# Two EGAT layers on one core: who gathers seven tiles of source rows in layer 2

## What is computed

```python
def _egat_conv(x, e, src, dst, W_ni, W_nj, W_fij, W_node, attn):
    f = (x @ W_ni.T)[src] + (x @ W_nj.T)[dst] + e @ W_fij.T
    f = leaky_relu(f, 0.2)
    score = f @ attn
    a = exp(score - segment_max(score, dst)[dst])
    a = a / segment_sum(a, dst)[dst]
    h = x @ W_node.T
    h_out = segment_sum(h[src] * a[:, None], dst)
    return h_out, f

h0, h1 = _egat_conv(x, e, src, dst, ...)          # layer 1
h0, h1 = relu(h0) + x, relu(h1) + e
h0b, _ = _egat_conv(h0, h1, src, dst, ...)        # layer 2
out = layernorm(x + h0b + x)
```

## Time and profile before

| | |
|---|---|
| time, median of three runs | 2155.59 us (2153.46 to 2156.14) |
| span of the profiled execution | 2849.0 us |
| PE busy in the span | 2104.0 us (74%) |
| GpSimd busy, nearly all in 1655 indirect transfers | 1576.3 us (55%) |
| VectorE busy | 1455.7 us (51%) |
| ScalarE busy, issuing not counted | 673.3 us (24%) |
| single-row transfers of ScalarE | 896 of 1 KB |
| mean granted clock of PE | 0.790 |

### The profile page before, as it was taken

One profiled execution on the slowest core, in us unless ns is written; L12 is line 12 of the kernel. 1 busy time (PEld: TensorE's weight loads), 2 busy tenths in 40 slices (PEclk: granted clock), 3 DMA queues, 4 the chain that ended last, 5 costly groups with the idle time before them and its releaser, 6 DMA issues.

```text
span 2849.0 us, 46360 instructions
## 1 busy us (share of the span) xinstructions
PE 2104.0 (74%) x10659; PEld 1469.1 (52%) x10816; DVE 1455.7 (51%) x5358; ACT 673.3 (24%) x1260; POOL 1576.3 (55%) x1664
## 2 busy tenths in 40 slices
PE   2377878777787778887854887776777877678778
PEld 2235555555555555555632555554555555455556
DVE  3334655555554555555721555554545555455556
ACT  0243333333333333333300111111111111111112
POOL 7326666666665656556263455555555556555650
PEclk7688887888787787787956877787877778778788
DMA  6646677666766666767543455555555555555551
GB/s 187 193 150 196 209 212 209 206 211 206 211 202 205 198 202 198 206 199 210 184 117 93 138 158 155 151 159 148 160 154 152 156 158 159 151 144 157 161 159 44
DMA packets 352361, 489.15 MB, mean 172 GB/s; under 512 B 115220, under 2 KB 217925, under 8 KB 352093
## 3 DMA queue, kind: packets, MB, share of 16 engines
q1 hardware_dynamic: 236803, 249.78, 29.2%
q0 software_dynamic: 78416, 212.69, 26.2%
q10 hardware_dynamic: 37017, 25.40, 3.0%
HBM read 409.00 MB, written 81.38 MB: 172 GB/s over the span
## 4 chain that ended last, share of the span: by engine, by line
PE 25%; another core or an unknown queue 23%; issue 21%; DVE 11%; ACTq 10%; ACT 4%; SPq 3%; DMA 1%; DVEq 1%
ACTq L755 6%; PE bSC L906 6%; PE pair L865 6%; PE pair L917 6%; DVE amat L1243 3%; PE pair L886 2%; ACTq L751 2%; DVE fT L1389 2%; ACT zc L715 1%; ACT onehot L767 1%; DVE h L1392 1%; PE pair L890 1%; ACT onehot L761 1%; SPq L438 1%
## 5 line engine op out<-in xcount | busy, mean ns | idle before, releaser
L585 POOL DMA_INDIRECT xsrc<-h_table,idx_slot x804 | 766.6, 953 | 562.3 <-issue 207.6
L585 POOL DMA_INDIRECT xsrc<-x_table,idx_slot x767 | 726.0, 947 | 551.7 <-issue 234.6
L906 PE MATMUL bSC<-fT,attn_at 128*32 128x128 f32 x3328 | 541.9, 317 | 204.7 <-DVE fT L1389 86.8
L715 ACT ACTIVATE zc<-pair 128x512 f32<-128x512 f32 x416 | 248.2, 597 | 1841.2 <-remote 1007.3
L865 PE MATMUL pair<-edge_in,wts 128*128 128x512 f32 x832 | 580.4, 785 | 23.4 <-issue 13.3
L917 PE MATMUL pair<-amat,xsrc 128*128 128x42 f32 x3328 | 532.2, 315 | 51.8 <-issue 49.8
L917 PEld LDWEIGHTS pair<-amat,xsrc 128*128 128x128 f32 x3328 | 497.0, 225 | 121.8 <-issue 110.1
L906 PEld LDWEIGHTS bSC<-fT,attn_at 128*32 128x32 f32 x3328 | 384.5, 127 | 304.4 <-issue 181.7
L1389 DVE TENSOR_TENSOR fT<-pair,zc 128x512 f32<-128x512 f32 x416 | 285.8, 687 | 423.7 <-ACT zc L715 219.7
L886 PEld LDWEIGHTS pair<-ident,xsrc 128*128 128x128 f32 x1600 | 251.3, 170 | 330.4 <-issue 328.7
L1243 DVE TENSOR_SCALAR amat<-iota_row,relc,wcol 128x42 f32<-128x42 f32 x1568 | 378.8, 319 | 14.8 <-DVE numT L1227 0.2
(11 more groups left out here) (170 smaller groups left out, 1408.9 us busy)
## 6 DMA issues: line engine op xcount, KB each, us to landing
edge_in<-eT SPq DMA_DIRECT2D x208, 256.0 KB
rel_bc<-relrow_g SPq DMA_DIRECT2D x416, 128.0 KB
h1T<-h SPq DMA_DIRECT2D x208, 256.0 KB
edge_in<-h1T SPq DMA_DIRECT2D x208, 256.0 KB
stage<-h_table ACTq DMA_DIRECT2D x896, 1.0 KB
window<-proj SPq DMA_DIRECT2D x416, 32.0 KB
xsrc<-h_table,idx_slot POOLq DMA_INDIRECT x824
xsrc<-x_table,idx_slot POOLq DMA_INDIRECT x767
```

Source lines behind the costliest of these rows:

```text
L585: pool.indirect_dma_start(xsrc[b][:, i, 0:width], None, table, bass.IndirectOffsetOnAxis(ap=idx_slot[b][:, i:i + 1], axis=0)).then_inc(L.g ...
L715: nc.scalar.mul(zc[s][:, :], bZ[s][:, :], SLOPE).then_inc(L.z_scaled, 1)
L906: last = mm(bSC[0:TC, 0:P], attn_at[:, L.n - 1, TC - 1 - t:2 * TC - 1 - t], fT[s][:, i * P:i * P + P], start=t == 0, stop=t == TC - 1)
```

## The change

GpSimd gathers all 32 tiles of every chunk in layer 2 too; `aided_rows`, its tiles, its index input and its semaphores are gone, PE's wait for a group has one form again, and ScalarE's loop goes over one chunk at a time, 21 times round, in both layers.

```diff
-AIDED = (CH - XB) // XB
-AID_AT = 2 * XB - 1
-ROWS_AT = [5, 7, 5, 6, 7, 6, 6, 7]
-def first_row(turn, g):
...
# GpSimd
-                        aided = L.n == 2 and not isinstance(c, int) and b == AID_AT % XB and g == GC - 1
-                        for i in range(g * TG, g * TG + TG - (SHORT if ends else aided)):
+                        for i in range(g * TG, g * TG + TG - (SHORT if ends else 0)):
# ScalarE
-                    if L.n == 2 and aid is not None:
-                        aided_rows(*aid, c, g)
-
-                def aided_rows(turn, u, begins, c, g):
...
-                turn(1, True, True, (2, -1, True))
-                turn(2, True, True, (0, 0, False))
-                turn(3, True, True, (1, 0, False))
-                with act.Fori(0, AIDED - 1) as j:
-                    turn(j * XB + 4, True, True, (2, j, True))
-                    turn(j * XB + 5, True, True, (0, j + 1, False))
-                    turn(j * XB + 6, True, True, (1, j + 1, False))
-                c = (AIDED - 1) * XB + 4
-                turn(c, True, True, (2, AIDED - 1, False))
-                for c in range(c + 1, CH):
+                for c in range(1, 4):
                     turn(c, True, True)
+                with act.Fori(4, CH - 1) as c:
+                    turn(c, True, True)
+                turn(CH - 1, True, True)
# PE
-                        elif L.n == 2 and b == AID_AT % XB and g == GC - 1:
-                            above(pe, L.aided_in, rounds * 16)
-                            pe.sem_inc(pe_passed, 1)
-                            earlier = (L.uses_before[b] + 1) * (16 * TG)
-                            pe.wait_ge(L.gathered[b][g], rounds * (16 * (TG - 1)) + earlier)
```

More of the change, by code:

```diff
@@ L40 @@
 SHORT = NT - TILES
-AIDED = (CH - XB) // XB
-AID_AT = 2 * XB - 1
-IN_RANGE = "src lies in [0, N)"
-ROWS_AT = [5, 7, 5, 6, 7, 6, 6, 7]
-def first_row(turn, g):
-    before = 0 if turn == 0 else ROWS_AT[GC - 1] + (turn - 1) * sum(ROWS_AT)
-    at = before + (0 if turn == 0 else sum(ROWS_AT[0:g]))
-    return at, max(0, min(ROWS_AT[g], P - at))
 class Layer:
@@ L99, in __init__ @@
         self.slab_stored = sem(f"slab_stored{n}")
-        self.line_in = sem(f"line_in{n}") if h1_out is None else None
-        self.rows_in = sem(f"rows_in{n}") if h1_out is None else None
-        self.aided_in = sem(f"aided_in{n}") if h1_out is None else None
         self.proj_stored = sem(f"proj_stored{n}") if h1_out is not None else None
@@ L141, in above, with program @@
         eng.wait_ge(sem, value)
-def program(nc, eT, xT, xrows, idxC, idxR, idxE, dstT, dstC, dst8, ends, w_fij1, w_ni1, w_nj1, w_node1, attn1,
+def program(nc, eT, xT, xrows, idxC, idxE, dstT, dstC, dst8, ends, w_fij1, w_ni1, w_nj1, w_node1, attn1,
             w_fij2, w_ni2, w_nj2, w_node2, attn2, out):
@@ L204, in program @@
         window = [sb(f"window{g}", [P, 3 * TG, P], bf16) for g in range(GS // 2)]
-        stage = sb("stage", [P, 2 * P])
-        line = sb("line", [1, P], i32)
         rel_bc = [sb(f"rel_bc{g}", [P, W], bf16) for g in range(GS)]
@@ L295, in program @@
         pe_passed, dve_passed, pool_passed = sem("pe_passed"), sem("dve_passed"), sem("pool_passed")
-        sp_passed, act_passed = sem("sp_passed"), sem("act_passed")
+        sp_passed = sem("sp_passed")
         const_in = sem("const_in")
@@ L706, in layer, with slot @@
             def layer(L, narrow):
-                def slot(c, g, front, soft, aid):
+                def slot(c, g, front, soft):
                     n, s = c * GC + g, g % 2
@@ L773, in copy_rows, with turn @@
                     nc.scalar.copy(xsT[s][:, :], bXT[:, :]).then_inc(L.xt_copied, 1)
-                def turn(c, front, soft, aid=None):
+                def turn(c, front, soft):
                     for g in range(GC):
-                        slot(c, g, front, soft, aid)
+                        slot(c, g, front, soft)
                 def whole_slab(k):
@@ L1489 @@
         "idxC": t(srcp.reshape(CH, TC, P).transpose(0, 2, 1)),
-        "idxR": t(srcp.reshape(CH, TC, P)[AID_AT:AID_AT + XB * AIDED:XB, TC - 1, :]),
         "idxE": t(srcp.reshape(CH, TC, P)[XB - 1, 0:SPEC].reshape(1, SPEC * P)),
```

## The result

The changed kernel takes 2166.4 us (median of four runs, 2162.8 to 2169.8) against 2155.9 for the kernel before in the same comparison; the ratio is 1.0043, with a 95% interval of 1.0030 to 1.0057. The medians differ by 10.6 us; the ratio gives 9.3 us, with an interval of 6.5 to 12.3. The forecast was 2163 us, in a range of 2144 to 2169. On two of the four chips that the experiments met, the kernel before takes about 2830 us (the long condition, mean granted clock of PE 0.78 to 0.80) instead of about 2155 (the usual condition, clock mostly 0.93 to 0.94), and the trace of the kernel before that stands above has the span and the clock of the long one. The changed kernel's profile was taken in the usual condition: its span of 2160.6 us agrees with its time.

A forecast was written before the change was run, and what follows sets the result against it. GpSimd's gathers were taken to pace both layers in the timed runs; seven more at 1.14 us add 8.0 to 2155.6, all else nothing, giving 2163.6, forecast as 2163 us since a part may hide; range 2144 to 2169, its own 2160 to 2167.

The forecast's parts named there:

- What bounds the kernel: Both layers, timed runs: GpSimd's gathers set the pace almost without a wait, four taking 4.56 us against 3.98 a slot.
- The duration of a gather: GpSimd's seven added gathers in layer 2: 1.14 us each, 8.0 us in all; 6.7 at 0.953, 8.3 at 1.179.
- ScalarE's work, counted at nothing: Removing 147 register loads and 896 rows, 551 us on ScalarE, saves nothing, hidden by the wait for GpSimd's rows.
- The loop's laps at nothing: ScalarE's loop, 21 laps instead of 6 in each layer: taken as nothing, bounded above by 123 us.
- The instruction fetch at the jump back: ScalarE's layer 2 loop refetches code at jump backs; the change removes six stops, some 4.1 us each, priced under faster.
- Rival A: Layer 2: other engines pace it too, so the seven gathers vanish in GpSimd's waits: 2155.6 us; chance 0.19.
- Rival B: Layer 2: ScalarE paces the slots between one `zc` and the next, so the change is faster, 2139 to 2118; chance 0.18.
- What would show it: Profile after: 831 gathers, no `stage` transfers, `zc` own-queue waits in layer 2 from 476 to below 50 us, no instruction packets.

The follow-up runs named there:

- the new trace: Kernel before, unedited, run once more for a profile in the usual condition: 2152.3 us, span 2150.1.
- all four comparisons with additional gathers: Changed kernel 1.0043; same gathers with ScalarE's row work kept 1.0041; changed kernel with ScalarE's three-chunk loop without rows 1.0049; changed kernel plus 21 gathers in layer 2 1.0155.
- rows and gathers: Kernel before with all ScalarE row work kept, but its tile copied to an unused place and GpSimd gathering all tiles: 2163.3 us, ratio 1.0041.
- left out: Changed kernel, but GpSimd leaves out the seven layer 2 tiles and nobody fetches them: 2153.9 us, ratio 1.0003.
- the pair at 29 gathers: 63 tiles left out of layer 2's gathers, long condition: changed kernel without rows 2720.0 us, 0.9623; kernel before with ScalarE's rows 2784.5 us, 0.9863.
- 21 left out: Changed kernel, but GpSimd leaves out the last tile of all 21 loop chunks in layer 2, fetched by nobody (1641 gathers): ratio 0.9910.
- the whole table: Seven kernels with 1641 to 1683 gathers against the kernel before, from 21 fewer than the changed kernel to 21 more: ratios 0.9910 to 1.0155.

## Why the prediction was right, point by point

- **What bounds the kernel.** Right in the usual condition, and the step that carried it was to hold the trace against the timed runs: 1655 gathers nearly fill the timed 2155.6 us, and the slots can run faster than four of them. The profile's own chain and waits did not show it, since they were taken in the other condition.
- **The duration of a gather.** The mechanism was right and this term mis-sized: "If those stretches keep their length, it takes at most 1.139 us" was no bound, since the idle stretches did not shrink by a quarter but from 192.5 to 17.9 us, the stretch behind the last gather from 74.4 to 44 us, and the gather kept its 1.25. That the gathers fill the time did not need a shorter gather: 1655 x 1.25 = 2069 us and the 66 us of such stretches that are left make 2135 of the 2150 us of the new trace. The value of 1.14 and the end at 1.179 are both too low; the trace's own 1.25, which I had put down as the upper end, is right, 7 x 1.25 = 8.8 us instead of 8.0. The forecast took off another 0.6 us for waits that might hide a part; no run shows such a part. The measured 2166.4 is within the forecast's own range of 2160 to 2167, and all four comparisons with additional gathers have 1.25 us within their intervals. That the wrong value did so little harm is due to the small number of gathers: seven times 0.11 us is less than the interval.
- **ScalarE's work, counted at nothing.** Right in the usual condition, by two pairs: rows and gathers against the changed kernel (1.0041, 1.0043), left out against before (1.0003). The cover is thicker than reckoned: the slot is 5.0 us, not 4.56. One argument for it was weak: that the slots of layer 2 are only 0.10 us longer than those of layer 1, "which have none". In layer 1 ScalarE makes the one-hots, twice 0.71 us a slot, so the two layers do not compare, and in the condition of that trace the work did cost time.
- **The loop's laps at nothing.** Right within a few us: 1.0049 and 1.0043 with 6 and 21 laps.
- **The instruction fetch at the jump back.** Right as an observation and without a price here: between 1300 and 1900 us the kernel before again has 35 instruction packets of that queue and the changed kernel none, and a stop is 4.1 us, yet the time does not show the six of them. In the reading of the earlier trace rows the prediction says that of 6.4 us of lateness 3.4 are for rows still to be issued; from 2021.1 to 2023.4 it is 2.3, and with that the 4.1 us come out.

```profile
q14 instruction: 35, 0.29, 0.1%
```

- **Rival A**, hidden: wrong, gathers count in both directions. **Rival B**, faster: wrong in the usual condition. On the chips in the long condition the change gains 0.8%, 22 us, and ScalarE's work costs time there (64 us in the pair at 29 gathers), as this rival said. Its price of 17 to 38 us takes in the 22; how much of it is stops at the jumps back and how much the rows' own issuing was not separated.
- **What would show it.** 811 + 20 gathers and no transfers to `stage`: so. `zc` on its own queue below 50 us in layer 2: so in the usual condition, where the waits of that stretch have no such row; in the long one it is 121.1. The ground, that a gather less in each chunk moves the time by about 1.1 us for each, holds as well: 1.39 for the 21 left out, 1.26 over the whole table. The shorter span came, but from the condition: in the long one the changed kernel still spans 2811.2 us.

What stays open: why some chips take 2830 us for a kernel that takes 2155 on others, and what sets the pace there. PE's granted clock is 0.79 in the mean instead of 0.94, and GpSimd waits 2 to 3 us at a time for PE's sums. No experiment was made on the cause.

No version that beats the kernel before came out of this. ScalarE could collect more than seven tiles only if its slot allowed it (0.6 + 1.5 + 2.8 = 4.9 us of 5.0 with seven rows), and sharing such rows with SP, or a smaller number in layer 1, was not tried.

## What to carry to other kernels

Before reading a profile's chain, set its span against the timed runs. Where they differ by a third, as here, the chain can be that of another condition; what one engine must do in all, held against the timed total, is then the better guide. Where one engine issues at a fixed rate almost without a pause, seven instructions less are worth seven times its period, and 580 us of work on a neighbour with room cost nothing as long as each slot's share fits. A gain bought that way can turn into a loss in another condition. And an engine that is missing from the chain may still not be free: that takes a run with fewer of its instructions to see.

## What the runs showed of the hardware

- GpSimd issues an indirect transfer of 128 rows every 1.25 us where nothing holds it (0.95 and a gap of 0.30), with rows of 512 bytes (a mean of 1.00 and the same gap) or 1 KB, and in both conditions of the chip, at a mean granted clock of PE of 0.79 and of 0.94.
- Loading five to seven registers from an index row took ScalarE 1.5 us in the median (0.7 to 2.5) in the usual condition, a single-row transfer 0.40 us (seven in 2.77); a tile of 128 rows costs it 83 us (21 x 1.509 + 128 x 0.40), 66 times a gather.
- A jump back of ScalarE's loop over three chunks stopped it for 4.1 us in the usual condition, with four packets on an instruction queue around it; between 1300 and 1900 us there were 35 such packets, none with the one-chunk loop, and one with the three-chunk loop without the rows.
- The kernel before took 2153 to 2156 us in three comparisons and 2828 to 2830 in two others, on two other chips; the profiles' granted clock was 0.93 to 0.94 in the first kind and 0.79 to 0.80 in the second.
